# Graph attention on one core: the first chunk of the next edge tiles is turned ahead of the messages, the head sums follow these directly, and block numbers are loaded one slot ahead

## The reference, cut to what matters

```python
N, E, DM, H, L = (1250, 20000, 768, 8, 2)      # 41250 edges with both directions and the loops
def gatv2_layer(x, Ws, bs, Wd, bd, attn, src, dst):
    hs = (x @ Ws + bs).reshape(N, H, HD)
    hd = (x @ Wd + bd).reshape(N, H, HD)
    hs_e = hs[src]
    e = jax.nn.leaky_relu(hs_e + hd[dst], SLOPE)
    logits = jnp.einsum('ehd,hd->eh', e, attn)
    m = jax.ops.segment_max(logits, dst, num_segments=N)
    ex = jnp.exp(logits - m[dst])
    s = jax.ops.segment_sum(ex, dst, num_segments=N)
    alpha = ex / s[dst]
    out = jax.ops.segment_sum(alpha[..., None] * hs_e, dst, num_segments=N)
    return jax.nn.elu(out).reshape(N, DM)
```

## Time and profile before

| | |
|---|---|
| time of the kernel before, median of 3 runs | 2622.97 us (2605.95 to 2636.16) |
| span of the profiled execution, first to last instruction | 2250.3 us |
| busy in the span | PE 96%, PEld 75%, DVE 75%, ACT 50%, POOL 40% |
| mean granted clock of TensorE | 0.986 of full |
| start of the first and last `line_up` of layer 0 | 545.6 and 1209.5 us |
| the same of layer 1 | 1435.1 and 2103.0 us |

### The profile page before, as it was taken

One profiled execution on the slowest core, in us unless ns is written; L12 is line 12 of the kernel. 1 busy time (PEld: TensorE's weight loads), 2 busy tenths in 40 slices (PEclk: granted clock), 3 DMA queues, 4 the chain that ended last, 5 costly groups with the idle time before them and its releaser, 6 DMA issues. The chain is left out here.

```text
span 2250.3 us, 86767 instructions
## 1 busy us (share of the span) xinstructions
PE 2154.9 (96%) x31007; PEld 1684.2 (75%) x31007; DVE 1678.2 (75%) x4435; ACT 1133.4 (50%) x2749; POOL 896.5 (40%) x849
## 2 busy tenths in 40 slices
PE   8999999998999999999997999899999999999798
PEld 4665555555888888888886655688888888888676
DVE  5546872344888888888887755588888888888884
ACT  1101200034666666666664314566666666666584
POOL 0000001022666566666652211466656656656121
PEclk9999999999999999999998999999999999999899
DMA  5002044144777777787774024587777777777421
GB/s 192 1 0 71 20 142 133 57 131 133 249 250 247 249 250 243 248 252 239 247 245 153 29 97 132 168 252 242 251 242 248 240 245 250 244 246 238 171 88 48
DMA packets 143398, 404.07 MB, mean 180 GB/s; under 512 B 21811, under 2 KB 81625, under 8 KB 143073
## 3 DMA queue, kind: packets, MB, share of 16 engines
q0 software_dynamic: 59584, 298.64, 41.0%
q1 hardware_dynamic: 79691, 93.00, 13.8%
q10 hardware_dynamic: 3828, 7.85, 1.0%
HBM read 370.77 MB, written 17.17 MB: 172 GB/s over the span
## 5 line engine op out<-in xcount | busy, mean ns | idle before, releaser
L502 ACT ACTIVATE at_relu<-at_turned,ah_attn_size 128x512 f32<-128x512 f32 x1092 | 716.2, 692 | 392.0 <-PE at_heads L578 363.4
L483 POOL DMA_INDIRECT at_rows<-table,ah_index x360 | 404.6, 1124 | 269.0 <-DVE ah_index L696 158.5
L483 POOL DMA_INDIRECT ah_room<-table,ah_index x352 | 399.8, 1136 | 260.8 <-DVE ah_index L696 174.3
L561 PE MATMUL at_turned<-ident,ah_room 128*128 128x128 f32 x2208 | 427.9, 280 | 2.3 <-issue 2.3
L559 PE MATMUL at_turned<-ah_place,dst_rows 96*128 96x128 bf16 x2208 | 407.7, 223 | 23.4 <-ACTq L537 19.2
L561 PE MATMUL at_turned<-ident,at_rows 128*128 128x128 f32 x2160 | 413.3, 277 | 1.7 <-issue 1.4
L559 PE MATMUL at_turned<-at_place,dst_rows 96*128 96x128 bf16 x2160 | 394.1, 222 | 2.2 <-issue 1.5
L686 DVE SCALAR_TENSOR_TENSOR sums<-sums,at_factor,at_total 128x97 f32 x1456 | 343.7, 310 | 1.4 <-DVE at_gap L751 0.7
L561 PEld LDWEIGHTS at_turned<-ident,ah_room 128*128 128x128 f32 x2208 | 318.1, 144 | 26.2 <-issue 1.7
L561 PEld LDWEIGHTS at_turned<-ident,at_rows 128*128 128x128 f32 x2160 | 307.8, 143 | 24.5 <-issue 2.2
L676 DVE TENSOR_TENSOR at_spread<-at_lined,at_weight 128x1024 f32<-128x1024 f32 x182 | 223.3, 1227 | 127.7 <-ACT at_weight L512 127.7
(11 more groups left out here) (317 smaller groups left out, 3179.7 us busy)
## 6 DMA issues: line engine op xcount, KB each, us to landing
at_flags<-run_flags SPq DMA_DIRECT2D x182, 64.0 KB
dst_rows<-pr_parts SPq DMA_DIRECT2D x76, 144.0 KB, 2.6
ah_place<-local_rows SPq DMA_DIRECT2D x92, 96.0 KB
at_place<-local_rows SPq DMA_DIRECT2D x90, 96.0 KB
table<-ah_room SPq DMA_DIRECT2D x20, 400.0 KB, 2.4
ah_room<-table,ah_index POOLq DMA_INDIRECT x368
at_rows<-table,ah_index POOLq DMA_INDIRECT x360
mx_w<-in_L_mix_W_qkv SPq DMA_DIRECT2D x4, 1152.0 KB, 11.8
```

Source lines behind the costliest of these rows:

```text
L483: pool.indirect_dma_start(rows[b][:, j, :], None, table, bass.IndirectOffsetOnAxis(index[b][:, j:j + 1], 0)).then_inc(gathered[b], 16)
L502: act.activation(relu[c][:], turned[chunk(b, c)][:], ACT.Relu, scale=attn_size[:, c:c + 1]).then_inc(bent, 1)
L561: last = pe.matmul(into, rows[b][:, j, c * P:(c + 1) * P], ident[:], is_transpose=True, start=False, stop=True)
```

## The change

In PE's `slot` three things move; nothing is added or taken away. Chunk 0 of m+2 goes from behind the messages to their front, so that the head sums of m+1 stand right behind the messages of m. The load of the block numbers goes from the start of the slot that uses them to the slot before, between the head sums and chunk 1. The two nested loops around `slot` become one over the macros; they were unrolled before too.

```diff
-                def slot(turn, head, message):
+                def blocks(turn):
+                    return places_of(nc, mybir.EngineType.PE, block_of, turn[0], 1) if turn else None
+
+                def slot(turn, head, message, at, coming):
                     if turn:
-                        at = places_of(nc, mybir.EngineType.PE, block_of, turn[0], 1)
+                        turn_chunk(*turn, at, 0)
                     if message:
                         for pair in range(2):
                             messages(message[0], message[1], pair)
-                    if turn:
-                        turn_chunk(*turn, at, 0)
                     if head:
                         sum_heads(head[0], head[1])
+                    after = blocks(coming)
                     if turn:
                         for c in range(1, 4):
                             turn_chunk(*turn, at, c)
...
+                    return after
...
-                for i in range(LOOPS):
-                    for b in range(UNROLL):
-                        slot(macro(i, b + 2), macro(i, b + 1), macro(i, b))
...
+                for m in range(2, NM):
+                    at = slot(macro(0, m), macro(0, m - 1), macro(0, m - 2), at, macro(0, m + 1) if m + 1 < NM else None)
```

More of the change, by code:

```diff
@@ L622, in slot @@
                         turn_chunk(*turn, at, 5)
+                    return after
                 pe.sem_inc(weights_ready, EXPS)
                 pe.sem_inc(added, ADDS)
-                slot(macro(0, 0), None, None)
-                slot(macro(0, 1), macro(0, 0), None)
-                for i in range(LOOPS):
-                    for b in range(UNROLL):
-                        slot(macro(i, b + 2), macro(i, b + 1), macro(i, b))
-                slot(macro(LOOPS, 2), macro(LOOPS, 1), macro(LOOPS, 0))
-                slot(None, macro(LOOPS, 2), macro(LOOPS, 1))
-                slot(None, None, macro(LOOPS, 2))
+                at = blocks(macro(0, 0))
+                at = slot(macro(0, 0), None, None, at, macro(0, 1))
+                at = slot(macro(0, 1), macro(0, 0), None, at, macro(0, 2))
+                for m in range(2, NM):
+                    at = slot(macro(0, m), macro(0, m - 1), macro(0, m - 2), at, macro(0, m + 1) if m + 1 < NM else None)
+                slot(None, macro(0, NM - 1), macro(0, NM - 2), None, None)
+                slot(None, None, macro(0, NM - 1), None, None)
                 pe.wait_ge(merge_ready, 1)
```

## The result

The changed kernel takes 2490.42 us (median of 4 runs, 2489.88 to 2491.19), the kernel before 2625.81 in the same comparison: a ratio of 0.949, 95% interval 0.945 to 0.953.

The account below looks back on a forecast made before the run. PE's own order was taken to set a 7.27 us slot; after the change a gather loop would bind at 7.23, so 180 slots save 7 us: 2623 - 7 = 2616 us, range 2562 to 2650.

Parts of the forecast that it names:

- the 373 us that lie between span and median stay: Whole kernel: time between profiled span (2250 us) and median (2623 us) was taken as unchanged, giving 2243 plus 373.
- The clock: PE's granted clock: at 9 tenths or more of full speed in 38 of 40 slices, so no part of the question.
- (a): PE's slot: two of four borders between full-width and strip work go, 0.39 us, 7.27 to 6.88; messages to head sums 0.
- the case with PE alone as the bound: Both layers' 180 slots: only the two saved borders count, 180 x 0.39 = -70 us, 2553 us.
- (b): PE's messages: their wait for the spread is gone, chunk 0 giving 0.80 us of cover; DVE then bounds at 6.97 us.
- What is late next: DVE's chain: 0.33 us can go before it sets the slot at 6.94, 6.97 with adds 0.03 later.
- (c): Register load of block numbers on PE's sequencer, behind the head sums: costs between 0 and 0.33 us, taken as 0.
- (d): Chunk 0's wait for gathers closes a two-slot loop of 3.76 + L, setting the slot at 7.23 us, above DVE's 6.97.
- a forecast of -54: Both layers' 180 slots without the gather loop binding: 180 x (6.97 - 7.27) = -54 us, 2569 us.
- L: Time from index copy to landing of the fourth gather: 9.1 to 12.3 us, taken as 10.7.
- the first rival: Gathers don't bind: -54 us, 2569, chance 0.33; marks: no gap ahead of chunk 0, index copies 6.9 to 7.0 us apart.
- gathers early enough: Same as the first rival: gathers land in time, L below 10.18 us, slot 6.97 us, 2569 us, chance 0.33.

Follow-up runs that it names:

- the quick trace: First recorded profile of the kernel before, nothing changed: span 2250 us, slots of 7.38 and 7.42 us, though the timed runs' median is 2623 us.
- the ordinary before: Second profile of the kernel before, no edit: span 2627.7 us, time 2629.4 us, slots of 9.45 and 9.56 us; ten-run median 2625.63 us, ratio 1.000.
- thin gathers: Changed kernel with each row's gather after the first round bringing 32 of 800 columns: 2491.01 us (one run).
- whole: Kernel before with messages in bf16, one load and one product each, uncut: 2474.59 us, ratio 0.944; again on another chip 2479.08 us, 0.947.
- halves: Kernel before with messages in bf16, each product cut in two (64 loads and 64 products a slot): 2604.06 us, ratio 0.972.
- quarters: Kernel before with messages in bf16, each product cut in four (128 loads and 128 products a slot): 2848.32 us, ratio 1.089.

## Why the prediction was wrong

**The step that failed** is the first one: that the span of 2250 and the cadence of 7.27 us were the kernel's, and that "the 373 us that lie between span and median stay" outside and unchanged. In an ordinary execution they lie inside, nearly 2.1 us in each of the 180 slots, as the two holds (in the messages and behind `turn_back`) and some slots at a low clock. The whole argument about 0.24 and 0.15 us at borders was worked out in slots that the timed kernel doesn't have. The rivals had none in which the missing 373 us were touched by the change, though it was the largest number on the page; the order of PE's work was just what moved them. The sums of the forecast come out as written; they are right for slots of 7.27 us.

Point by point:

- The clock, set aside as "no part of this question": true of the quick trace, where both layers run at 1.00. In the ordinary before it is 0.98 and 0.97 there, and, by the estimate above, up to 31 us of the gain are its own.
- (a) Borders. Messages to head sums cost nothing, as taken: the first load of the head sums starts at 898.12, before the messages' group ends at 896.81 + 1.38 = 898.19. The two borders are worth little in an ordinary execution: putting two of them back cost 16 us, against the 70 of the case with PE alone as the bound.
- (b) The wait for the spread is gone, as said: what the message loads wait for it falls from 15.0 us in the ordinary before to 1.7. "What is late next" wasn't DVE's chain at 6.97: it was the hold, met at the adds.
- (c) The load costs nothing in the new order, as taken (2491.5 without its move, 2490.4 with it). In the old order it costs 20 us, a case that I hadn't priced.
- (d) The loop through the gathers was the step that turned a forecast of -54 into one of -7. It doesn't set the pace. Nothing stands between chunk 5 and chunk 0 of the changed kernel: the loads go on 0.17 us apart across the border (895.74, 895.91), the mark set for the first rival. Gathers of 4% of the bytes changed nothing (2491.0). L itself was well guessed at 10.7: by the landing events of the gathers' semaphores it is 10.5 us in the quick trace (median, layer 0) and 10.9 in the changed kernel, 8.6 with thin gathers. What was off is the rest of the loop and the slot. The hold lies inside the loop: from chunk 0's first load to the index copy it takes 901.26 - 895.91 = 5.35 us instead of 3.61 (3.76 without the signal), so with slots of 8.73 the loop would bind from L = 2 x 8.73 - 5.35 - 0.15 = 11.96. That is near: the last landing that the trace has comes 0.88 us before chunk 0's first load (median), and in 12 of 182 macros directly before it, by 0.12 us. Without holds the loop would give (3.76 + 10.5) / 2 = 7.13 us, an estimate that no run here can test.
- The rival "gathers early enough" had the right sign and one of its two marks, no gap ahead of chunk 0; the index copies are 8.6 us apart (901.26 and 909.86), not 6.9 to 7.0. It had 2569 instead of 2490, and its mechanism (two borders) isn't where the gain came from.

**What is shown, and what isn't.** Shown: the order alone has the gain; the late signal ahead of the weights goes and a longer wait at the adds comes, 293 against 177 us; the holds follow the order, and in the old order the number of small products (whole, halves, quarters), as does the time. Shown not to cause the holds: gather bytes (one run of each kernel), zeros in the rows, instruction fetch. Spacing by increments didn't prevent them (one run). Not shown: which part of the chip holds PE, why the hold comes after 59 message loads in one order and in the head sums in the other, why the signal of `turn_back` is late in the old order, with full-width chunks between it and the last burst, and why one execution in dozens had almost no holds.

One rival stands untested: the writing of the profile's own records. Every run of the changed kernel and of the experiments has a span and a clock on record, so each was recorded, and the times of both kernels may be times under recording. The traces themselves differ on this point. The quick one has 13.1 semaphore events per us of its span, and 11255 of the 11648 landing events of the gathers; all 17 others, whatever their kernel, have 8.5 to 9.4 events per us, the ordinary before 7614 of those landings and the changed kernel 6895. So where there are holds, records are missing too. The Trainium skill, page NOTIFIC — Programmer's Manual, section When the ring fills, says that a full record queue by default loses the record that didn't fit, and that in another mode it stalls its producer. Missing records agree with the first; no run here shows that the second is at work, and none varies the recording.

**A better version.** The changed kernel with bf16 messages takes 2431 us, 59 less than the changed kernel's 2490 and 7% less than before, if the truncation of the sources in the messages can be borne. In f32 none of the orders tried beats the changed kernel (order alone is equal to it).

## What to carry to other kernels

Set the span of a profile against the median before reading anything in it. Where they differ by far more than the 1.7 us of the ordinary before, the trace may show an execution unlike the timed ones, and it can't say in which stages the missing time lies; profile again, or give a chance to every case in which the change touches it. Look at the granted clock of the stages and not only at its mean: 0.974 against 0.984 hid 27 slow slots against two. Before a pause put down to "issue" is read as the engine's own, look up in the program what its next instruction waits for (line 589 here waits for ACT). When an engine's signals come late while its records look punctual, ask which consumer meets the delay: a reordering that lets the delay fall on a shorter chain is worth more than the borders it saves. And count instructions, not only array time, where products are small: an f32 product stands in the trace as two.

## What was unexpected of the hardware

- The same kernel ran once at 7.4 us a slot, with a span of 2250 us, and in its second profile at 9.5, with 2628; no timed run came below 2598.
- PE pauses for 0.53 to 0.65 us at a time within messages and head sums, first behind 59, 78 and 81 small loads in the slots shown; in the order of before the signal of `turn_back` comes up to 2.9 us behind its recorded end.
- Around long holds the granted clock fell to 0.50, mostly for 3.4 us; in the ordinary before the slots in which it fell took 10.1 to 13.7 us, where those at the full clock take 9.2 on average.
- Twelve semaphore increments on PE in each slot cost 98 us over the kernel, 45 ns for each.
- Rolling PE's program up, 51 instruction packets in place of 265, made it 2.5% slower.
- Cutting each bf16 product in four cost 369 us, though the array's columns stayed the same.
